# A one-core transformer layer on Trainium2: loads split over two DMA queues, and other orders in the first and the last slots

## What is computed

```python
q, k, v = heads(x @ wq + bq), heads(x @ wk + bk), heads(x @ wv + bv)
attn = softmax(q @ k.T * 48 ** -0.5 + adj)              # adj: one 128x128 bias a graph
x1 = rmsnorm(x + (attn @ v) @ wo + bo) * alpha1 + gamma1
y = rmsnorm(x1 + silu(x1 @ w1 + b1) @ w2 + b2) * alpha2 + gamma2   # w1: 384x1536
out = layernorm(x + y)
```

## Time and profile before

| | |
|---|---|
| median of 3 runs | 2967.57 us (2967.24 to 2967.73) |
| profiled execution | 2968.35 us, of it span of the instructions 2966.6 us |
| PE busy | 2923.2 us, 99% of the span |
| DVE, ACT, POOL busy | 1974.3, 1441.6, 697.8 us |
| mean granted TensorE clock | 0.995 |
| chain that ended last | PE 96%, DVE 1%, ACT 1%, SP 1% |

### The profile page before, as it was taken

One profiled execution on the slowest core, in us unless ns is written; L12 is line 12 of the kernel. 1 busy time (PEld: TensorE's weight loads), 2 busy tenths in 40 slices (PEclk: granted clock), 3 DMA queues, 4 the chain that ended last, 5 costly groups with the idle time before them and its releaser, 6 DMA issues.

```text
span 2966.6 us, 62752 instructions
## 1 busy us (share of the span) xinstructions
PE 2923.2 (99%) x25216; PEld 2871.9 (97%) x25216; DVE 1974.3 (67%) x3621; ACT 1441.6 (49%) x4260; POOL 697.8 (24%) x968
## 2 busy tenths in 40 slices
PE   7999999999999999999999999999999999999998
PEld 6999999999999999999999999999999999999998
DVE  5766666666666676666666666666666667666665
ACT  5455455454554454544545545545445445454442
POOL 0222222222222222222222222222222222222222
PEclk9999999999999999999999999999999999999999
DMA  5211211211212112112122121121121211211200
GB/s 163 74 57 47 69 53 50 69 47 56 68 35 69 56 47 69 52 52 69 41 63 59 45 68 54 50 69 48 55 69 36 68 56 47 69 52 51 63 28 28
DMA packets 155491, 171.93 MB, mean 58 GB/s; under 512 B 18624, under 2 KB 155200, under 8 KB 155200
## 3 DMA queue, kind: packets, MB, share of 16 engines
q1 hardware_dynamic: 155200, 167.91, 19.1%
HBM read 92.35 MB, written 25.17 MB: 40 GB/s over the span
## 4 chain that ended last, share of the span: by engine, by line
PE 96%; DVE 1%; ACT 1%; SPq 1%; issue 0%; POOL 0%; DMA 0%; POOLq 0%; ACTq 0%; DVEq 0%
PE ps_work L450 48%; PE ps_rows L518 27%; PE ps_rows L450 6%; PE ps_att L462 4%; PE ps_att L471 4%; PE ps_att L482 2%; PE ps_att L486 2%; PE ps_work L560 2%; PE ps_rows L560 1%; SPq L331 0%; ACT probs L704 0%; DVE w_s L864 0%; SPq L383 0%; ACT squares L719 0%; DVE neg_max L876 0%
## 5 line engine op out<-in xcount | busy, mean ns | idle before, releaser
L450 PE MATMUL ps_work<-x1T,w_s 128*128 128x256 f32 x6912 | 847.7, 283 | 2.9 <-ACT h_raw L760 2.2
L450 PEld LDWEIGHTS ps_work<-x1T,w_s 128*128 128x128 f32 x6912 | 835.6, 188 | 3.5 <-ACT h_raw L760 2.4
L518 PE MATMUL ps_rows<-w_s,h 128*128 128x384 f32 x4608 | 822.2, 339 | 10.7 <-DVE x1T L922 7.0
L518 PEld LDWEIGHTS ps_rows<-w_s,h 128*128 128x128 f32 x4608 | 801.4, 189 | 18.7 <-issue 7.4
L760 ACT ACTIVATE h_raw<-ps_work,b_col 128x256 f32<-128x256 f32 x768 | 322.7, 471 | 478.5 <-PE ps_work L450 471.3
L704 ACT ACTIVATE probs<-probs,neg_max 128x128 f32<-128x128 f32 x1024 | 396.0, 388 | 238.5 <-DVE neg_max L876 238.5
L946 DVE TENSOR_TENSOR h<-h_raw,h 128x512 fp32r<-128x512 f32 x384 | 359.3, 936 | 13.2
L944 DVE CAST h<-h_raw 128x512 fp32r<-128x512 f32 x384 | 165.7, 431 | 302.7 <-ACT h_raw L760 302.2
L419 POOL TENSOR_TENSOR x_last<-x_last,rows 128x768 f32<-128x768 f32 x64 | 117.7, 1839 | 773.8 <-PE ps_att L462 773.8
L407 POOL TENSOR_SCALAR mean_sq<-sum_sq 128x1 f32<-128x1 f32 x256 | 69.0, 270 | 975.4 <-ACT squares L719 975.3
L450 PE MATMUL ps_work<-wv_s,xT 128*128 128x384 f32 x1152 | 235.2, 348 | 2.1 <-ACT qk_flat L740 1.2
(11 more groups left out here) (86 smaller groups left out, 3440.7 us busy)
## 6 DMA issues: line engine op xcount, KB each, us to landing
qk<-qk_flat SPq DMA_DIRECT2D x384, 96.0 KB, 2.4
x_in<-in_x SPq DMA_DIRECT2D x64, 384.0 KB, 3.2
x_res<-in_x SPq DMA_DIRECT2D x64, 384.0 KB, 3.9
x_last<-in_x SPq DMA_DIRECT2D x64, 384.0 KB, 3.2
out<-y SPq DMA_DIRECT2D x63, 384.0 KB, 2.5
bias<-in_adj SPq DMA_DIRECT2D x64, 128.0 KB, 3.8
qk<-qk_flat SPq DMA_DIRECT2D x128, 64.0 KB, 2.1
qk<-qk_flat SPq DMA_DIRECT2D x128, 32.0 KB, 2.0
```

What stands on the lines that cost most here:

```text
L450: mm = pe.matmul(ps_out, stationary(sta), moving(mov), start=(i == 0), stop=(i == n - 1))
L518: mm = pe.matmul(ps_rows[b][:, 0:d], h[:, sta, m, b * P:(b + 1) * P], w2_s[:, mov, m, :], start=(m == 0 and i == 0), stop=(m == fc - 1 and ...
```

## The change

- ScalarE issues the three loads of wq and the three bias columns at its start; SP issues wk, wv and the rest.
- ScalarE and VectorE split wq before the transposed x of slot 0 (`queries`), wk after it (`keys`).
- In slot 1 SP issues the first five of the ten moves and ScalarE the other five, after waiting for all of `qk_ready`. Later slots are unchanged.
- In slots 2 and 3 VectorE takes the transposed x before the first norm of x1.
- In slot 4 the wait for the last weight unit becomes one wait for each of the 12 chunks of `down`.
- In slots 65 and 66 the last third of x1T goes to `ps_work[1]` (new helper `x1_third`) and waits for an earlier `silu` in place of `res1_ready[1]`; `down` of graph 1 waits only for its own group's x1T; the transposes of the probabilities of graph 0 move behind that `down`.
- In the same slots VectorE does `split_h` of pair 0 before, and of pair 1 inside, the norm of graph 1.

```diff
-        splits_due = {(0, "projections"): range(wv_from), (0, "values"): range(wv_from, wo_from),
+        splits_due = {(0, "queries"): range(wk_from), (0, "keys"): range(wk_from, wv_from), (0, "values"): range(wv_from, wo_from),
...
+        def x1_third(g):
+            return ps_work[1] if ending(g + LAG_FF1) else ps_rows[1]
...
             load_x(0)
-            for n in range(wv_from):
-                load_weights(n)
-            for col, src in ((bq_col, bq), (bk_col, bk), (b1_col, b1)):
-                sp.dma_start(col[:], src.rearrange("(c p) -> p c", p=P)).then_inc(cols_loaded, 16)
-            for n in range(wv_from, wo_from):
+            for n in range(wk_from, wo_from):
                 load_weights(n)
...
-                    for p0, c, to, pair, n in moves:
+                    for p0, c, to, pair, n in moves if t > LAG_PROJ else moves[:len(moves) // 2]:
...
                 if b == 1:
-                    pe.wait_ge(x1T_lo[1], through(g + 1 if ending(g + LAG_FF2) and live(g + 1) else g))
+                    pe.wait_ge(x1T_lo[1], through(g))
                 for m in range(fc):
...
+                    if b == 0 and g == 0:
+                        pe.wait_ge(weight_split, up_units + m + 1)
...
                 if ending(g + LAG_FF1):
-                    pe.wait_ge(res1_ready[1], through(g))
+                    pe.wait_ge(silu_ready[fc // 2 - 1], through(g - 1))
...
-                transpose_rows(ps_rows[1], x1[:, 1 - parity], (2,), x1T_done[1])
+                transpose_rows(x1_third(g), x1[:, 1 - parity], (2,), x1T_done[1])
...
                     if live(g_ff1):
                         transpose_x1(g_ff1, parity)
-                    if live(g_attn):
-                        transpose_probs(g_attn, 0)
                     down(g_ff2, 1)
                     if live(g_attn):
-                        transpose_probs(g_attn, 1)
+                        for b in range(PAIR):
+                            transpose_probs(g_attn, b)
...
-                    if t == LAG_FF2:
-                        pe.wait_ge(weight_split, len(units))
...
         def _(act):
+            for n in range(wk_from):
+                act.dma_start(staging(n), units[n][0][0][2]).then_inc(stage_loaded[staged_at(n)], 16)
+            for col, src in ((bq_col, bq), (bk_col, bk), (b1_col, b1)):
+                act.dma_start(col[:], src.rearrange("(c p) -> p c", p=P)).then_inc(cols_loaded, 16)
...
+                if t == LAG_PROJ:
+                    for i in range(3):
+                        act.wait_ge(qk_ready[i], through(g_proj))
+                    for p0, c, to, pair, n in moves[len(moves) // 2:]:
+                        act.dma_start(qk[to:to + n, :, pair, :], qk_flat[p0:p0 + n, :, c, :]).then_inc(qk_moved, 16)
...
-                    norm1(g_attn, 0, parity)
                     transposed_lo(t, 0, ps_work[1], xT_hi, xT, xT_lo)
                     transposed_lo(t, 1, ps_rows[0], xT_hi, xT, xT_lo)
+                    norm1(g_attn, 0, parity)
...
                     residual2(g_ff2, 1, parity)
+                    if live(g_ff1):
+                        split_h(g_ff1, 0)
                     norm2_and_stats(g_ff2, 1)
+                    if live(g_ff1):
+                        split_h(g_ff1, 1)
                     layer_norm(g_ff2, 1)
                     if live(g_ff1):
-                        for m in range(fc // 2):
+                        for m in range(2, fc // 2):
                             split_h(g_ff1, m)
```

More of the change, by code:

```diff
@@ L256, in build_layer @@
             unit([(0, P, w2[m * P:(m + 1) * P, :])], [w2_s[:, part, m, :] for part in (HI, LO)])
+        wk_from = kd
         wv_from, wo_from, w1_from, w2_from = 2 * kd, proj_units, out_units, up_units
@@ L767, in slot_program @@
                 g_proj, g_attn, g_ff1, g_ff2 = t - LAG_PROJ, t - LAG_ATTN, t - LAG_FF1, t - LAG_FF2
+                if t == 0:
+                    weights_hi(t, "queries")
                 if t == 1:
@@ L782, in slot_program @@
                         transposed_hi(g_ff1, 0, ps_work[0], x1T_done, x1T, x1T_hi)
-                        transposed_hi(g_ff1, 1, ps_rows[1], x1T_done, x1T, x1T_hi)
+                        transposed_hi(g_ff1, 1, x1_third(g_ff1), x1T_done, x1T, x1T_hi)
                     weights_hi(t, "middle")
@@ L842, in slot_program @@
                     transposed_hi(t, 1, ps_rows[0], xT_done, xT, xT_hi)
-                weights_hi(t, "projections")
+                weights_hi(t, "keys")
                 weights_hi(t, "values")
@@ L990, in slot_program @@
                         transposed_lo(g_ff1, 0, ps_work[0], x1T_hi, x1T, x1T_lo)
-                        transposed_lo(g_ff1, 1, ps_rows[1], x1T_hi, x1T, x1T_lo)
+                        transposed_lo(g_ff1, 1, x1_third(g_ff1), x1T_hi, x1T, x1T_lo)
                     weights_lo(t, "middle")
@@ L1066, in slot_program @@
                     norm1(g_attn, 0, parity)
+                if t == 0:
+                    weights_lo(t, "queries")
                 if live(t):
@@ L1069, in slot_program @@
                     transposed_lo(t, 1, ps_rows[0], xT_hi, xT, xT_lo)
-                weights_lo(t, "projections")
+                weights_lo(t, "keys")
                 if t == 0:
```

## The result

The changed kernel took 2943.83 us (median of 4 runs, 2943.52 to 2945.12), the kernel before, in the same series of runs, 2967.65 us: a ratio of 0.992, interval 0.9907 to 0.9933. The prediction was 2942.9, range 2938.5 to 2950.

The account below looks back on a forecast made before the run. PE, without gaps in steady slots, bounds the kernel; only gaps and low clock near both ends can be won. 6.8-0.3+4.0+7.9+4.0+2.3 = 24.7 us off the median 2967.57 gives 2942.9 us, range 2938.5 to 2950.

Parts of the forecast that it names:

- First moves: Slots 0 to 2: with moves issued on two queues the scores start at 23.8 us, 4.9 us earlier.
- The rival of bytes: Start bound by bytes: moves on two queues wait behind weights, the 6.8 us goes, time 2949.7; chance 0.07.
- the columns would cost nothing: At the start the bias columns compete with wk: zero cost, up to 0.5 us against if wq comes late.
- Clock in slot 2: Behind the first moves, 1.7 us of low-clock loss remains of 3.65: 1.9 us won, bounds 0 and 3.65.
- x ahead of the norm: Slots 2 and 3: PE waits for ScalarE's hi part before slot 3's projection, 0.3 us lost.
- Slot 4: `down` starts without the wait for w2, new waits follow on queries and keys: 4.0 us won, bounds 2.5 to 6.1.
- Slot 65: From `down` 0 to `up`, the 4.60 us wait for x1T and low clock go: 7.9 us won.
- slot 66: From `down` 0 to `up`, 17.3 us become 13.3: 4.0 us won.
- its `up`: Inside slot 66's `up`, the 2.21 us gap goes because pairs 0 and 1 are split earlier: 2.3 us won.
- Steady slots: They stay at 45.43 us; the rival that they get longer, at 0.6 us a slot 2979 us, has chance 0.03.
- the first rival: One descriptor generator for both queues: ten issues take 6.5 us however split, 6.8 becomes 2.3, time 2947.4; chance 0.15.

Follow-up runs that it names:

- e12_again: The changed kernel once more, unaltered, in a second series of runs: 2945.68 us.
- e3_moves_sp: The changed kernel with all ten first moves issued by SP again, ScalarE still issuing wq and the columns: 2948.86 us.
- e6_norm_first: The changed kernel with the norm of graph 0 ahead of the transposed x again on VectorE, in slots 2 and 3: 2946.66 us.
- e8_no_split: The changed kernel, but in slots 65 and 66 VectorE splits all of h after both norms again: 2949.6 us.
- e9_slots: The changed kernel with slot 2's norms moved behind slot 3's row maxima, and awaited work put first in slots 4 and 65: 2943.65 us.
- e2_ends_only: The kernel before with the change of slots 65 and 66 and nothing else: 2954.18 us.

## Why the prediction was right, and which terms were off

The forecast's mechanism happened in each of its parts, and the trace's gain of 24.5 us stands against a sum of 24.7. That they agree to 0.2 us is in part luck: the first moves fell 1.15 us short, and the other terms together gave about 0.9 more than forecast. With the trace of `e12_again` (span 2944.4 us) the gain is 22.2. By terms:

- **First moves, 4.9 us predicted, 3.75 measured.** Three steps were mis-sized. PE was to start 0.3 us earlier and started 0.7 later: I had the split of wq moved ahead of x, and not that x and wk now come beside wq (x at 4.90 for 4.06 us) and that wq's last unit, not x, would then be last. The keys were to be out at 17.9 and were at 18.45. The landing was to stay 2.36 us with 0.2 for two streams and was 3.37, at a DMA share of 0.97, as the moves crowd each other and the next x loads beside them. Part of that error was hidden by another: the 2.36 us of the earlier trace rows run from the start of the last issue (26.28) and the 6.53 of the earlier trace rows end with it (26.89), so the sum 17.9+3.3+2.36 counts 0.6 us twice. Counted once it gives 23.2 us in place of 23.8, and 24.94 was measured. That SP would be free at 16.4 was right (16.77), and so was the halved issue time. The rival of bytes was thus true for one microsecond of its 6.8, and the bytes were not those of weights. That the columns would cost nothing held in this trace, and not in that of `e3_moves_sp`.
- **Clock in slot 2, 1.9 predicted, 1.95 measured** (scores to queries 5.92 us in place of 7.87). The agreement is luck of the trace: in `e12_again` the scores start 2.89 us earlier than before, not 3.75, and from scores to queries it is 7.19 us, which wins 0.68. The bounds that I gave this term (0 to 3.65) were real, and it decides the last digits. Of the 5.70 us won up to the queries 0.12 are lost again in the rest of slot 2.
- **x ahead of the norm, -0.3 predicted, -0.28 measured** between the two traces, -0.29 in `e6_norm_first`.
- **Slot 4, 4.0 predicted, 4.40 measured.** 0.84 of it in `up`, where I had counted the gap of 0.57 and not PE's restart behind it; 3.56 from the scores to the x1 transposes, which started at 120.25 before, not at the 120.42 of my sum. Predicted waits 1.65 and 0.6 us, measured 1.05 and 0.53: the first queries were ready 5.4 us after `down` (105.90 less 100.46) and not 5.9.
- **Slot 65, 7.9 and 7.85; slot 66, 4.0 and 4.2; its `up`, 2.3 and 2.5.** The stall of 0.75 us at the first `silu` was 0.52. `e8_no_split` shows what the splits were worth to slot 65 too, 1.68 us beside that, which my sum held inside its 7.9 without a number of its own.
- **Steady slots** stayed (45.42 us); the drift over sixty of them is 0.2 us in favour.

What the traces didn't decide is the time of a typical run. The median of the second series, 2945.68, is 2.8 us above the forecast, that of the first 0.9, both inside the forecast's own bounds of 2939 to 2947. The forecast counted on the shorter of the spells, as the two gaps of similar length before had it, and the runs have both. The first series' chip isn't on record, so a part of the difference between the series could be the chip's; `e6_norm_first` has times at both ends on one chip (2943.70, and 2946.47 to 2946.88 in the other three).

The Trainium skill, Perfetto Trace Analysis, section "DMA Instruction — HWDGE (DVE, Sync)", was the source beside the first rival, and the trace disagrees with it as far as it was read there: two engines issued moves at the same time at 0.66 and 0.72 us each, against 0.65 alone. The Trainium skill, DMA: Bandwidth & Descriptors, section "Issuing engines are not separate DMA queues", says that several issuers save the sequencer's time and share the DMA engines, and the trace agrees: the sequencer's time was saved, and the landing, which shares the engines, grew from 2.36 to 3.37 us.

## What to carry to other kernels

When many small DMAs in a row bound a step, give half to an idle engine's queue, but first look whether the first queue is free in time, and allow for a longer landing of moves that come twice as fast: of the 2.9 us of issue time saved here, one went back into it. A gap of TensorE is to be costed with the lower clock behind it and less the waits that it hides: in slot 4 that was 3.75 plus 1.32 less 2.0 us. And when an edit takes work from ahead of a late step, look where it goes: ahead of the next late step it wins nothing, as in slot 3 of `e9_slots`.

## What the runs showed of the hardware that I had not expected

- **Loads of four-byte pieces delay the issue behind them.** Behind three loads of four-byte pieces (the largest 6 KB) the next issue on the same queue took 3.04 us in place of 0.38, though it was an unrelated transfer; in the kernel before, wv's three issues behind the columns took 3.37 us, and without columns ahead of them 1.67 in the one after. On ScalarE's queue, with nothing issued behind them, the same loads cost their issuer 0.46 to 0.78 us each, but the last landed 9.1 us after its issue, and 11.4 in `e3_moves_sp`.
- **The first rise of the clock isn't at a fixed time.** In two executions of one program it came at 13.01 and 14.83 us after the first instruction, and between 11.80 and 14.97 in the seven that share slots 0 and 1.
- **Spells at the lower level came in three lengths**, 3.41, 6.83 and 10.24 us. The last is that of the first moves before: it began at 26.06 us, 2.6 us ahead of the scores, and the earlier trace rows shows the 7.61 us of it in which PE worked. The same gap of 3.58 us in the same program was followed by either of the first two, and so was the gap of 3.69 us in slot 4, 3.41 before and 6.83 in `e2_ends_only`. The stalls of 1.68 and 2.21 us in `e8_no_split` were followed by none, the gap of 2.37 us of the kernel before by one.
